# Eight small bias loads issued from SyncE instead of GpSimd at the start of a perceiver block

## The chip, the cores and the metric

The kernel runs on one core of one Trainium2 chip. The metric is the device time of one execution in microseconds (us), as the median of several runs. Profiled executions are read through a trace in which PE is TensorE, PEld its weight loads, DVE VectorE, ACT ScalarE, POOL GpSimd and SP SyncE. A name that ends in q (SPq, POOLq) is an engine's own queue of instructions, from which DMAs are issued.

## What is computed

One layer in float32 over x of 16 x 64 x 256 and a context of 16 x 1601 x 256: cross-attention, self-attention with rotary positions, and a mixture of 8 experts with one expert for each token and a capacity of 128.

```python
x = x + xattn(layernorm(x), ctx, ctx, Wq, bq, Wk, bk, Wv, bv, Wo, bo)   # 16 heads of 16
x = x + attn(layernorm(x), Wqkv, bqkv, Wout, bout)                      # 16 heads, rotary
x = x + ffn(layernorm(x), wg, W, b)                                     # top 1 of 8 experts
```

The biases are not zero. The loads that the change moves bring four of them: `be`, the experts' bias (8 x 256), and parts of `brows`, which holds bv, bo, bqkv and bout one after the other.

## The kernel before

Each of the five engines runs a program of its own; they meet at semaphores alone. The cross-attention goes through 16 contexts, one after the other. For each, PE makes keys (eight units, `L790`, 6 matmuls each, 512 or 65 columns wide) and values (seven units, `L799`, up to 12 matmuls of 256 columns), as sums of three products of bf16 parts. A unit goes to one of four PSUM banks for the first context, of two after that, and a unit may start only when the one before it in its bank has been read out: for keys by ACT (`khigh`, L1191) and then DVE (`klow`, L1458). SP copies the key rows by DMA into `kstack` (L487, three loads for each of eight pairs of heads), PE multiplies them with the queries (`ps_front`, L822), DVE takes maxima (L1475); then come the scores (L850), the exponentials (ACT, L1213), their low parts (POOL, L622) and the weighted values (L874).

The order on each engine is written out by hand as strings of letters (`PE_PROGRAM`, `ACT_PROGRAM`, `DVE_PROGRAM`, `POOL_PROGRAM`, and `FIRST_ORDER` for the units of the first context). Units 15 and 16 of the first context are the query tile 0 (its transposes L755, its product L765), unit 17 holds the transposes of query tile 1. PE runs 15, 16, then key units 0 to 5, unit 17, key unit 6, value units 8, 9, 10, and then the first two `ps_front` products.

What a query tile needs: DVE's moments (`query_moments` L1369, `query_variance` L1375 and L1377), then POOL's inverse root (L547) and normed rows `h0` (L551), then PE's transposes (L755). `mv0` and `h0` have one buffer each, so DVE's variance of the next tile waits for POOL's `h0` of this one (L1374), and POOL's next `h0` for PE's transposes. In the head, POOL does tile 0, the four quarters of the first context's low part (`clow`, L565), ten DMA issues (L572 to L580), and then tiles 1 and 2.

SP issues the loads of contexts and weights (L455 to L463), two loads of ones into rows 96 and 97 of `kstack` (L464, L465; each moves two rows of 25,632 bytes), then waits for the first query tile, writes it to DRAM (`q_blocks`, L471, two DMAs), waits until both have landed (`q_sent`, L478), and only then loads `qstack` (L480) and `kstack` (L487) in order.

The semaphore `ld_be` counts the eight small loads. It is waited for in `fold(0)` on POOL (L592; it runs after the first context's values, and the trace has it at 39.6 us), and by ACT in `rooms_empty` (L1227), after the sixteenth context. `ones_set` counts three fills by POOL, one of them that of `bias3` with zeros, into which six of the loads write.

Of the kernel before, what the change touches and what calls it, by code (L numbers as in the profile page):

```python
# [18 lines left out]
P = 128  # L19
D = 256  # L20
# [11 lines left out]
E = 8  # L32
# [178 lines left out]
def build(nc, x, ctxT, wqT, wkT, wvT, bqk, woT, wqkv, wout, brows, wg, weT, be, consts, ones2, out):  # L211
# [3 lines left out]
    with ctx:  # L215
        def sb(name, shape, dt=f32):
            return ctx.enter_context(nc.sbuf_tensor(name, shape, dt))

        def sem(name):
            return ctx.enter_context(nc.semaphore(name))  # L220
# [34 lines left out]
        bvcol = sb("bvcol", [P, 2, KT])  # L255
# [21 lines left out]
        bias3 = sb("bias3", [SEL, 3 * D])  # L277
# [75 lines left out]
        for rows, n in ((stats, 6), (mv, 2), (ve, 1), (rs, 1)):  # L353
# [22 lines left out]
        ones_set, st0_rdy, mv0_rdy, var0_rdy, rs0_rdy, bq4_rdy = (  # L376
            sem(n) for n in ("ones_set", "st0_rdy", "mv0_rdy", "var0_rdy", "rs0_rdy", "bq4_rdy"))
# [30 lines left out]
        ld_be, picked_rdy, pick_rdy, bias_rdy, wrot_rdy, we_rdy, vbd_set = (  # L408
            sem("t_" + n) for n in ("ld_be", "picked", "pick", "bias", "wrot", "we", "vbd"))
# [43 lines left out]
        def _(sp):  # L453
# [9 lines left out]
            sp.dma_start(cbuf[1][:, :, :], ctxT[1].rearrange("(k p) n -> p k n", p=P)).then_inc(c_loaded[1], 16)  # L463
            sp.dma_start(kstack[0][96:98, :, :].rearrange("p a n -> p (a n)").bitcast(f32), ones2).then_inc(ld_ones, 16)  # L464
            sp.dma_start(kstack[1][96:98, :, :].rearrange("p a n -> p (a n)").bitcast(f32), ones2).then_inc(ld_ones2, 16)  # L465

            def send_queries(t):

                wait_free(sp, [query_unit(t, NREAL + 1)])
                for n in range(2):  # L470
                    sp.dma_start(q_dram[n, 2 * t:2 * t + 2].rearrange("b p n -> p b n"),  # L471
                                 qbd[n][:, :, :].rearrange("p (b o) c -> p b (o c)", o=KT)).then_inc(q_sent, 16)
# [64 lines left out]
        def _(pool):  # L537
# [30 lines left out]
            for quarter in range(4):  # L568
                low_context(0, quarter)

            for r in range(3):
                pool.dma_start(bias3[32 * r:32 * r + E, 2 * D:3 * D], be).then_inc(ld_be, 16)  # L572
                pool.dma_start(bias3[32 * r:32 * r + 1, 0:2 * D],
                               brows[2 * D:4 * D].rearrange("(p n) -> p n", p=1)).then_inc(ld_be, 16)
            pool.dma_start(bvcol[:, 0, :], brows[0:D].rearrange("(k p) -> p k", p=P),
                           allow_slow_non_contiguous=True).then_inc(ld_be, 16)
            pool.dma_start(bvcol[:, 1, :], brows[4 * D:5 * D].rearrange("(k p) -> p k", p=P),
                           allow_slow_non_contiguous=True).then_inc(ld_be, 16)
            pool.dma_start(wqkv_sb[:, :, :], wqkv.rearrange("(k p) n -> p k n", p=P)).then_inc(ld_t, 16)
            pool.dma_start(wg_sb[:, :, :], wg.rearrange("(k p) n -> p k n", p=P)).then_inc(ld_t, 16)  # L580

# [34 lines left out]
            def low_prob(b, k):  # L616
                _, n = keys_of(k)
                i = NCH * b + k
                slot = i % NPAR
                pool.wait_ge(exp_done, 2 * (i + 1))  # L620
                wait(pool, pv_done, i - NPAR + 1)
                nc.gpsimd.tensor_tensor(plow[slot][0:n, :], prob[slot][0:n, :], p_high(slot, 0, HP * P)[0:n],  # L622
                                        ALU.subtract).then_inc(plow_gps, 1)
# [523 lines left out]
        def _(act):  # L1147
# [55 lines left out]
            def exponentials(b, h):  # L1203
                k, e = divmod(h, 2)
                _, nn = keys_of(k)
                i = NCH * b + k
                slot = i % NPAR
                act.wait_ge(score_done, 2 * NCH * b + h + 1)
                if h == 0 and b == 0:
                    act.wait_ge(v0_low, VUNITS)  # L1210
                if e == 0:
                    wait(act, pv_done, i - NPAR + 1)
                nc.scalar.activation(prob[slot][0:nn, e * 512:e * 512 + 512], ps_score[0:nn, h % NSB, :], ACT.Exp)\  # L1213
                    .then_inc(exp_done, 1)
# [143 lines left out]
        def _(dve):  # L1358
# [80 lines left out]
            def low_prob(b, k):  # L1439
                _, nn = keys_of(k)  # L1440
                i = NCH * b + k
                slot = i % NPAR
                dve.wait_ge(exp_done, 2 * (i + 1))
                wait(dve, pv_done, i - NPAR + 1)
                nc.vector.tensor_tensor(plow[slot][0:nn, :], prob[slot][0:nn, :], p_high(slot, 0, HP * P)[0:nn],
                                        ALU.subtract).then_inc(plow_dve, 1)
# [22 lines left out]
            def maximum(b, m):  # L1469
                dve.wait_ge(m_done, MUNITS * b + m + 1)  # L1470
                ps = ps_front[:, front_pos(m) % 2, :]
                unit = max_unit(m)
                _, hp, n = unit[0]
                _, nn = piece(n)
                nc.vector.reduce_max(maxes[:, hp:hp + len(unit), n],  # L1475
                                     ps[:, 0:len(unit) * nn].rearrange("p (h k) -> p h k", k=nn), AX.X).then_inc(m_free, 1)
                if m % (MUNITS // 2) == MUNITS // 2 - 1:
                    shift(b, m // (MUNITS // 2))
# [339 lines left out]
```

## Time and profile before

| | us |
|---|---|
| median of 3 runs | 725.64 |
| lowest, highest | 723.0, 725.91 |
| the profiled execution, its own time | 724.36 |
| its span, first to last instruction | 722.2 |
| mean granted TensorE clock | 0.991 |

Times in rows count from the span's start. In a timeline, a row is the start, the duration, the engine, the line and the operation; what stands in brackets is how long the engine sat idle before it and which work ended that. In the chain of work that ended last, a row is a start, a duration and what ran; it is followed back from the last instruction to the first. PEclk is the granted TensorE clock as a share of 2.4 GHz.

### The profile page before, as it was taken

The numbers are of one execution on the slowest core, as the hardware profiler recorded it, in microseconds if no ns is written. First come the engines' busy times: TensorE is split into PE (matmuls) and PEld (weight loads), VectorE is DVE, ScalarE is ACT, GpSimd is POOL, SyncE is SP. The second block draws the span as 40 slices with busy tenths as digits, with TensorE's granted clock in tenths as the row PEclk, the third lists the DMA queues.
The fourth block names the chain that finished last, engine by engine and source line by source line (L and its number), as shares of the span: only waits on it lengthen the run. The fifth ranks groups of instructions, "written<-read, shape, count | busy, mean of one in ns | idle before, by whom it ended". The sixth has DMA issues, their size and how long they took to land.

```text
span 722.2 us, 21443 instructions
## 1 busy us (share of the span) xinstructions
PE 679.1 (94%) x8591; PEld 514.8 (71%) x8647; DVE 540.3 (75%) x1110; ACT 449.9 (62%) x881; POOL 557.2 (77%) x378
## 2 busy tenths in 40 slices
PE   4889999999999999999999999999999998898796
PEld 2547776868776878687868786878686886676573
DVE  5598778868877887788768776877686978777636
ACT  2436765766666667666766666666666786666430
POOL 7986997999698969896989698869885789622313
PEclk9999999999999999999999999999999999999889
DMA  9486054444754354445444445454444330000124
GB/s 312 126 228 187 21 131 144 113 134 94 221 135 147 90 155 108 146 95 157 107 146 100 147 104 153 100 150 105 148 96 108 87 119 2 1 1 9 52 74 131
DMA packets 45658, 84.57 MB, mean 117 GB/s; under 512 B 8525, under 2 KB 28405, under 8 KB 45557
## 3 DMA queue, kind: packets, MB, share of 16 engines
q1 hardware_dynamic: 43848, 80.26, 40.7%
q0 software_dynamic: 1008, 2.40, 1.1%
q8 instruction: 69, 1.13, 0.7%
q10 hardware_dynamic: 704, 0.55, 0.3%
q14 instruction: 29, 0.23, 0.1%
HBM read 37.02 MB, written 6.82 MB: 61 GB/s over the span
## 4 chain that ended last, share of the span: by engine, by line
PE 79%; POOL 6%; issue 5%; DVE 5%; ACT 2%; DMA 2%; SPq 0%; POOLq 0%; DVEq 0%; ACTq 0%
PE ps_kv L799 17%; PE ps_kv L790 16%; PE ps_out L874 11%; PE ps_score L850 11%; PE ps_front L822 11%; POOL plow L622 3%; POOL clow L565 1%; PE ps_score L898 1%; PE ps_out L890 1%; PE ps_kv L898 1%; DVE klow L1458 1%; DVE maxes L1475 1%; PE ps_front L831 1%; PE ps_front L898 1%; DMA kstack<-khigh 1%
## 5 line engine op out<-in xcount | busy, mean ns | idle before, releaser
L622 POOL TENSOR_TENSOR plow<-prob 128x1024 bf16<-128x1024 f32 (+1 forms) x200 | 376.2, 1901 | 63.2 <-ACT prob L1213 60.7
L1475 DVE TENSOR_REDUCE maxes<-ps_front 128x1 f32<-128x512 f32 (+1 forms) x416 | 268.3, 665 | 70.7 <-PE ps_front L822 68.8
L1213 ACT ACTIVATE prob<-ps_score 128x512 f32<-128x512 f32 (+1 forms) x416 | 231.7, 595 | 48.1 <-PE ps_out L874 29.9
L850 PE MATMUL ps_score<-qstack,kstack 98*128 98x128 bf16 (+1 forms) x1664 | 140.1, 219 | 0.9 <-ACT prob L1213 0.7
L874 PE MATMUL ps_out<-vstack,prob 128*128 128x65 bf16 (+1 forms) x1664 | 137.9, 194 | 1.0 <-POOL plow L622 0.6
L850 PEld LDWEIGHTS ps_score<-qstack,kstack 98*128 98x128 bf16 (+1 forms) x1664 | 111.1, 98 | 38.6 <-ACT prob L1213 1.6
L874 PE MATMUL ps_out<-vstack,plow 128*128 128x65 bf16 (+1 forms) x1664 | 137.0, 192 | 0.0
L822 PE MATMUL ps_front<-kstack,qstack 96*128 96x512 bf16 (+1 forms) x512 | 135.7, 333 | 1.0 <-DMA kstack<-khigh 0.6
L874 PEld LDWEIGHTS ps_out<-vstack,prob 128*128 128x128 bf16 (+1 forms) x1664 | 118.5, 97 | 2.8 <-POOL plow L622 1.5
L874 PEld LDWEIGHTS ps_out<-vstack,plow 128*128 128x128 bf16 (+1 forms) x1664 | 112.7, 98 | 3.5
L1191 ACT ACTIVATE khigh<-ps_kv,bcol 128x512 bf16<-128x512 f32 (+1 forms) x123 | 72.9, 594 | 63.1 <-PE ps_kv L790 62.1
L565 POOL TENSOR_TENSOR clow<-cbuf 128x801 bf16<-128x801 f32 (+1 forms) x64 | 96.9, 1532 | 17.6 <-DMA cbuf<-in_ctxT 8.0
L799 PE MATMUL ps_kv<-w_hi,cbuf 128*128 128x256 bf16 (+1 forms) x402 | 109.6, 273 | 0.3 <-DVE vstack L1465 0.3
L799 PE MATMUL ps_kv<-w_hi,clow 128*128 128x256 bf16 (+1 forms) x402 | 109.5, 272 | 0.0
L799 PE MATMUL ps_kv<-w_lo,cbuf 128*128 128x256 bf16 (+1 forms) x402 | 109.4, 272 | 0.0
L1458 DVE SCALAR_TENSOR_TENSOR klow<-ps_kv,bcol,khigh 128x512 bf16<-128x512 f32 (+1 forms) x123 | 76.1, 629 | 40.1 <-ACT khigh L1191 39.9
L1199 ACT CAST vstack<-ps_kv 128x512 bf16<-128x512 f32 (+1 forms) x105 | 58.3, 556 | 71.6 <-PE ps_kv L799 71.1
L790 PE MATMUL ps_kv<-clow,w_hi 128*128 128x512 bf16 (+1 forms) x245 | 78.2, 332 | 4.6 <-DVE klow L1458 2.0
L790 PE MATMUL ps_kv<-cbuf,w_lo 128*128 128x512 bf16 (+1 forms) x246 | 80.6, 340 | 0.2 <-issue 0.2
L1465 DVE TENSOR_TENSOR vstack<-ps_kv,vstack 128x512 bf16<-128x512 f32 (+1 forms) x105 | 67.4, 643 | 0.2
L790 PE MATMUL ps_kv<-cbuf,w_hi 128*128 128x512 bf16 (+1 forms) x201 | 63.4, 331 | 2.8 <-DVE klow L1458 2.8
L822 PEld LDWEIGHTS ps_front<-kstack,qstack 96*128 96x128 bf16 x512 | 44.5, 97 | 17.0 <-DVE maxes L1475 2.8
(277 smaller groups left out, 844.6 us busy)
## 6 DMA issues: line engine op xcount, KB each, us to landing
kstack<-khigh SPq DMA_DIRECT2D x256, 100.1 KB, 2.2
cbuf<-in_ctxT SPq DMA_DIRECT2D x15, 1601.0 KB, 7.7
kstack<-klow SPq DMA_DIRECT2D x128, 100.1 KB, 2.2
qstack<-q_blocks SPq DMA_DIRECT2D x48, 64.0 KB, 2.7
q_blocks<-qbd SPq DMA_DIRECT2D x16, 128.0 KB, 2.0
cbuf<-in_weT SPq DMA_DIRECT2D x2, 1024.0 KB, 7.2
slot_x<-att_all SPq DMA_DIRECT2D x1, 1024.0 KB, 10.5
vstack<-slot_x SPq DMA_DIRECT2D x4, 256.0 KB, 3.5
```

What stands on the lines that cost most here:

```text
L565: nc.gpsimd.tensor_tensor(clow[par][:, k, a:a + n], cbuf[par][:, k, a:a + n], c_high(par, k, a, n), ALU.subtract).then_inc(clow_done, 1)
L622: nc.gpsimd.tensor_tensor(plow[slot][0:n, :], prob[slot][0:n, :], p_high(slot, 0, HP * P)[0:n], ALU.subtract).then_inc(plow_gps, 1)
L790: mm = nc.tensor.matmul(ps[:, 0:nn], w[0][:, k, t * P:(t + 1) * P], rhs, start=(j == 0), stop=(j == len(terms) - 1))
L799: mm = nc.tensor.matmul(ps[0:nn, a * D:(a + 1) * D], lhs, w[1][:, k, :], start=(j == 0), stop=(j == len(terms) - 1))
L822: mm = nc.tensor.matmul(ps[:, at:at + nn], qstack[par][0:96, q_at(hp), :], kstack[par][0:96, hp, n0:n0 + nn], start=True, stop=True)
L850: mm = nc.tensor.matmul(ps_score[0:nn, h % NSB, j * P:(j + 1) * P], kstack[par][0:98, hp, n0:n0 + nn], qstack[par][0:98, q_at(hp), :], sta ...
L874: mm = nc.tensor.matmul(o, lhs, vstack[par][0:nn, k, hp, 0:OW], start=(k == 0 and part == 0 and hp % 4 == 0), stop=(k == NCH - 1 and part ...
L1191: nc.scalar.activation(khigh[:, t, n0:n0 + nn], kv_bank(b, u)[:, 0:nn], ACT.Identity, bias=bcol[:, 1, t:t + 1]).then_inc(high_done, 1)
L1213: nc.scalar.activation(prob[slot][0:nn, e * 512:e * 512 + 512], ps_score[0:nn, h % NSB, :], ACT.Exp)\
L1458: nc.vector.scalar_tensor_tensor(klow[:, t, n0:n0 + nn], kv_bank(b, u)[:, 0:nn], bcol[:, 1, t:t + 1], khigh[:, t, n0:n0 + nn], ALU.add, AL ...
L1465: nc.vector.tensor_tensor(v[:, :, :, 32:64], kv_bank(b, u)[0:rows, 0:nch * D].rearrange("p (c h d) -> p c h d", c=nch, h=HP), v[:, :, :, 0 ...
L1475: nc.vector.reduce_max(maxes[:, hp:hp + len(unit), n], ps[:, 0:len(unit) * nn].rearrange("p (h k) -> p h k", k=nn), AX.X).then_inc(m_free, 1)
```

## The change

POOL no longer issues the six loads into `bias3` and the two into `bvcol`; SP issues them, after the loads of ones and before it waits for the first query tile. SP gets a wait for `ones_set`, so that `bias3` has been filled before. Semaphores, bytes and consumers stay as they were. The loads of `wqkv_sb` and `wg_sb` remain on POOL. Lines after 465 have numbers 9 higher in the kernel after, and those after 578 one higher.

```diff
@@ SP @@
             sp.dma_start(kstack[1][96:98, :, :].rearrange("p a n -> p (a n)").bitcast(f32), ones2).then_inc(ld_ones2, 16)
+            sp.wait_ge(ones_set, 3)
+            for r in range(3):
+                sp.dma_start(bias3[32 * r:32 * r + E, 2 * D:3 * D], be).then_inc(ld_be, 16)
+                sp.dma_start(bias3[32 * r:32 * r + 1, 0:2 * D],
+                             brows[2 * D:4 * D].rearrange("(p n) -> p n", p=1)).then_inc(ld_be, 16)
+            sp.dma_start(bvcol[:, 0, :], brows[0:D].rearrange("(k p) -> p k", p=P),
+                         allow_slow_non_contiguous=True).then_inc(ld_be, 16)
+            sp.dma_start(bvcol[:, 1, :], brows[4 * D:5 * D].rearrange("(k p) -> p k", p=P),
+                         allow_slow_non_contiguous=True).then_inc(ld_be, 16)
@@ GpSimd, after low_context(0, quarter) @@
-            for r in range(3):
-                pool.dma_start(bias3[32 * r:32 * r + E, 2 * D:3 * D], be).then_inc(ld_be, 16)
...
-            pool.dma_start(bvcol[:, 1, :], brows[4 * D:5 * D].rearrange("(k p) -> p k", p=P),
-                           allow_slow_non_contiguous=True).then_inc(ld_be, 16)
             pool.dma_start(wqkv_sb[:, :, :], wqkv.rearrange("(k p) n -> p k n", p=P)).then_inc(ld_t, 16)
```

On POOL before, from the first context's low part (`clow`) to the normed rows (`h`) of query tile 1, the instructions in their order are:

```order
L565 TENSOR_TENSOR clow<-cbuf 128x800 x2
L572 DMA bias<-in_be 8x256
L573 DMA bias<-in_brows 1x16x32
L572 DMA bias<-in_be 8x256
L573 DMA bias<-in_brows 1x16x32
L572 DMA bias<-in_be 8x256
L573 DMA bias<-in_brows 1x16x32
L575 DMA bvcol<-in_brows 128x2x1
L577 DMA bvcol<-in_brows 128x2x1
L579 DMA wqkv_sb<-in_wqkv 128x2x768
L580 DMA wg_sb<-in_wg 128x2x8
L547 TENSOR_TENSOR rs<-ve,half_neg 128x1
```

and on POOL now, at the same place:

```order
L574 TENSOR_TENSOR clow<-cbuf 128x800 x2
L580 DMA wqkv_sb<-in_wqkv 128x2x768
L581 DMA wg_sb<-in_wg 128x2x8
L556 TENSOR_TENSOR rs<-ve,half_neg 128x1
L560 TENSOR_SCALAR h<-x_all,mv,rs 128x256
```

Eight issues have left POOL, and the load of `wqkv_sb` comes right behind the low part. On SP now, between the loads of ones and the write of the first query tile (before, the first row was followed at once by the last two):

```order
L465 DMA kstack<-in_ones 2x6408
L468 DMA bias<-in_be 8x256
L469 DMA bias<-in_brows 1x512
L468 DMA bias<-in_be 8x256
L469 DMA bias<-in_brows 1x512
L468 DMA bias<-in_be 8x256
L469 DMA bias<-in_brows 1x512
L471 DMA bvcol<-in_brows 128x2x1
L473 DMA bvcol<-in_brows 128x2x1
L480 DMA q_blocks<-qbd 128x2x256 x2
L489 DMA qstack<-q_blocks 32x4x256 x3
```

The eight issues now stand in SP's queue ahead of `q_blocks`.

## Rows read from the trace of the kernel before

**Rows 1.** The page: busy us of the engines; the chain's shares by engine.
```profile
PE 679.1 (94%) x8591; PEld 514.8 (71%) x8647; DVE 540.3 (75%) x1110; ACT 449.9 (62%) x881; POOL 557.2 (77%) x378
...
PE 79%; POOL 6%; issue 5%; DVE 5%; ACT 2%; DMA 2%; SPq 0%; POOLq 0%; DVEq 0%; ACTq 0%
```
**Rows 2.** The chain that ended last, 0 to 60 us: start, duration, what.
```profile
13.77 0.74 POOL bias L572
...
28.63 1.31 PE ps_kv L799 x12
...
47.66 1.34 PE ps_kv L790 x6
```
**Rows 3.** Timeline of POOL, 0 to 25 us: start, duration, line, operation.
```profile
13.71 0.79 POOL L572 DMA_DIRECT2D bias<-in_be  x1
...
18.79 0.74 POOL L579 DMA_DIRECT2D wqkv_sb<-in_wqkv  x1
...
20.22 0.62 POOL L547 TENSOR_TENSOR rs<-ve,half_neg 128x1 f32<-128x1 f32 x1
20.95 1.22 POOL L551 TENSOR_SCALAR h<-x_all,mv,rs 128x256 f32<-128x256 f32 x1
```
**Rows 4.** Timeline of DVE, 17 to 23 us.
```profile
17.18 0.15 DVE L1377 TENSOR_SCALAR ve<-mv 128x1 f32<-128x1 f32 x1
...
22.27 0.18 DVE L1375 BATCH_NORM_AGGREGATE mv<-st 128x2 f32<-128x6 f32 x1 [3.29 <-POOL h L551]
...
22.56 0.28 DVE L1458 SCALAR_TENSOR_TENSOR klow<-ps_kv,bcol,khigh 128x65 bf16<-128x65 f32 x1
```
**Rows 5.** Timeline of PE, 19 to 30 us.
```profile
19.57 0.39 PE L790 MATMUL ps_out<-cbuf,w_lo 128*128 128x512 bf16 x1
22.22 0.44 PE L755 MATMUL ps_kv<-cst,h 128*128 128x128 f32 x2 [2.26 <-POOL h L551]
...
29.78 0.60 PE L822 MATMUL ps_front<-kstack,qstack 96*128 96x512 bf16 x2
```
**Rows 6.** Timeline of SP's queue, 0 to 26 us: its DMA issues.
```profile
3.66 3.03 SPq L463 DMA_DIRECT2D cbuf<-in_ctxT  x1
...
7.15 0.24 SPq L465 DMA_DIRECT2D kstack<-in_ones  x1
14.90 0.91 SPq L471 DMA_DIRECT2D q_blocks<-qbd  x2
21.95 1.28 SPq L480 DMA_DIRECT2D qstack<-q_blocks  x3
...
24.55 1.23 SPq L487 DMA_DIRECT2D kstack<-khigh  x2
```
**Rows 7.** SP's waits, 14 to 24 us: for what, total, times, longest.
```profile
SPq L480 <- DMA q_blocks<-qbd: 6.1, 1, 6.1
```
**Rows 8.** The page's DMA issues: count, KB each, us from issue to landing.
```profile
kstack<-khigh SPq DMA_DIRECT2D x256, 100.1 KB, 2.2
```
**Rows 9.** DMA answer of 0 to 40 us: the load of wqkv_sb.
```profile
wqkv_sb<-in_wqkv POOLq DMA_DIRECT2D x1, 768.0 KB, 4.7
```
**Rows 10.** DMA answer of 14 to 16 us: packets, what all queues moved.
```profile
DMA packets 130, 0.83 MB, mean 416 GB/s; under 512 B 0, under 2 KB 0, under 8 KB 130
```
**Rows 11.** DMA answer of 17.5 to 19.8 us: packets, MB, share of 16 engines.
```profile
q1 hardware_dynamic: 4, 0.05, 12.4%
```
**Rows 12.** The same view, POOL's queue, 16.2 to 17.6 us.
```profile
q0 software_dynamic: 128, 0.02, 8.4%
```
**Rows 13.** The same view, POOL's queue, 18.8 to 19.8 us.
```profile
q0 software_dynamic: 35, 0.00, 22.9%
```
**Rows 14.** By stretch: busy of PE, PEld, DVE, ACT, POOL; PEclk, DMA, GB/s.
```profile
22.80:26.20 3.40, 2.99 (x9) 1.36 (x11) 2.02 (x6) 0.73 (x2) 3.30 (x4) 0.50 0.64 160
26.20:29.80 3.60, 3.60 (x35) 3.23 (x34) 1.08 (x2) 2.38 (x5) 3.60 (x3) 1.00 0.63 148
```
**Rows 15.** Engines by stretch, the same columns, 36.0 to 45.7 us.
```profile
36.00:45.70 9.70, 7.52 (x46) 3.72 (x46) 9.56 (x24) 4.12 (x9) 7.46 (x9) 1.00 0.74 164
```

More of the change, by code:

```diff
@@ L569, in _ @@
                 low_context(0, quarter)
-            for r in range(3):
-                pool.dma_start(bias3[32 * r:32 * r + E, 2 * D:3 * D], be).then_inc(ld_be, 16)
-                pool.dma_start(bias3[32 * r:32 * r + 1, 0:2 * D],
-                               brows[2 * D:4 * D].rearrange("(p n) -> p n", p=1)).then_inc(ld_be, 16)
-            pool.dma_start(bvcol[:, 0, :], brows[0:D].rearrange("(k p) -> p k", p=P),
-                           allow_slow_non_contiguous=True).then_inc(ld_be, 16)
-            pool.dma_start(bvcol[:, 1, :], brows[4 * D:5 * D].rearrange("(k p) -> p k", p=P),
-                           allow_slow_non_contiguous=True).then_inc(ld_be, 16)
             pool.dma_start(wqkv_sb[:, :, :], wqkv.rearrange("(k p) n -> p k n", p=P)).then_inc(ld_t, 16)
```

## The prediction

> **What bounds the kernel now.** I read the page first. PE is busy for 679.1 us, and the chain of work that ended last is PE in 79% of the span and POOL in 6% [rows 1]. So time is won or lost where PE waits, and it has to be a wait in the head, since the change touches nothing else. Next, the chain in order of time. Behind POOL's four `clow` pieces it runs through POOL's DMA issues [rows 2], and these end only when POOL starts the inverse root for query tile 1 at 20.22 [rows 3]. DVE had the variance for it at 17.18 + 0.15 = 17.33 [rows 4]. Third, PE's timeline. Its key unit 5 ends at 19.57 + 0.39 = 19.96. Then it sits idle for 2.26 us until 22.22, until POOL's `h` (20.95 + 1.22 = 22.17) is there [rows 3, 5]. The small issues are the cause of that idle time.
>
> The next dependence on PE's path is the first `ps_front` product, at 29.78 [rows 5]. It wants `qstack` and the first head pair of `kstack`, which SP can ask for only when both writes of `q_blocks` have landed. SP issues these at 14.90, and waits 6.1 us for them, until 21.95 [rows 6, 7]. The third load of the first head pair starts its issue at 24.55 [rows 6] and lands some 2.2 us later [rows 8]: 26.75. Here the wait has 29.78 - 26.75 = 3.03 us of slack. That slack is what a faster POOL can use up; behind it stands a DMA queue.
>
> **What is removed.** Eight issues on POOL, from 13.71 to 18.79: 5.08 us [rows 3]. `wqkv_sb` and `wg_sb` follow in 20.22 - 18.79 = 1.43 us, so POOL is free for tile 1 at 13.71 + 1.43 = 15.14. It then waits for DVE, until 17.33. So of 5.08 us only 20.22 - 17.4 = 2.8 us move anything. The root and `h` take 22.17 - 20.22 = 1.95 us, and `h` is ready at 19.35, ahead of PE's 19.96. PE's idle 2.26 us goes entirely.
>
> **What PE does with it.** Unit 6 behind the transposes needs its bank, free after DVE's short `klow`, which stands in DVE's order behind a `mv` that waited 3.29 us for the old `h` [rows 4]. That `klow` ends at 22.84 before, 0.67 behind `h`; now at 19.35 + 0.67 = 20.02. The transposes take 0.44 [rows 5], so unit 6 starts at about 20.4. At full clock a key unit takes 1.34 and a value unit 1.31 [rows 2]: PE would reach the first `ps_front` at 20.4 + 1.34 + 3 x 1.31 = 25.7. That is 4.1 us earlier than 29.78; more than the 2.26 because units 6 and 8 ran at PEclk 0.50 from 22.8 to 26.2 in the trace [rows 14], behind the idle stretch that is gone. 4.1 us is the ceiling of the gain.
>
> **What holds it back.** If `q_blocks` landed as before, `kstack` would be there at 26.75 and the gain would be 3.0. But two things come ahead of it in the DMA engines.
>
> First, `wqkv_sb`: its issue moves from 18.79 to 13.71. Now its 768 KB [rows 9] run at 21 to 23.5 us, behind `q_blocks`; they will run from about 15 on, beside the second context and the two loads of ones. At the 416 GB/s of that stretch [rows 10] they are 786 / 416 = 1.9 us of every engine. In the stretch from 17.5 to 19.8 us SP's queue has two long packets (and two small ones), 12.4% of 16 engines, or 2 of 16 for 2.3 us [rows 11]: the loads of ones, on two engines alone, and `q_blocks` is complete only when these two engines have come to it. They have no gap in which to take 1.9 us more. I take the full 1.9; the bounds are 0 (another queue's packets slip in at no cost beside the slow long packets) and 1.9.
>
> Secondly, the small loads themselves, now ahead of `q_blocks` in SP's queue. The nearest rows are POOL's. With the six bias loads 128 packets took 8.4% of 1.4 us x 16, or 15 ns each [rows 12]; with the `bvcol` loads 35 packets took 22.9% of 1.0 x 16, or 105 ns each [rows 13]. The `bvcol` loads have 2 x 256 elements of 4 bytes, 32 for each engine. As packets of their own, they cost 32 x 15 ns = 0.5 us at the low end and 32 x 105 ns = 3.4 us at the high end. A packet of POOL's queue may hold many elements, so an element should cost far less than 105 ns, and those 15 ns are a mean over packets of up to 1 KB. I take 0.2 us, and keep 0 to 3.4 for the range.
>
> The Trainium skill, "DMA: Bandwidth & Descriptors", section "Rules for kernel authors", says that a strided last dimension is lowered to one descriptor per element, and that spreading DMAs over issuing engines saves the sequencer's time alone. The trace agrees with the second (5.08 us of POOL's time, the same engines busy); no row here shows the first for SP's queue. By the first, the price would be between the two ends above.
>
> SP's own issue time is covered. Its slowest issue took 3.03 us while earlier loads were outstanding, and its last ends at 7.15 + 0.24 = 7.39; it is idle until 14.90 [rows 6]. Eight issues at POOL's own price are 5.08 us and end at 12.5; even with one more stall of 3.03 they end at 15.5, 0.6 us behind 14.90, and `q_blocks` would still queue behind the ones loads. The wait for `ones_set` is met by 2 us. Behind it stand only these loads and the query writes. The loads' consumers come at 39.6 us and near the end: no wait there.
>
> **The sum.** `q_blocks` has landed at 21.95 + 1.9 + 0.2 = 24.05, and the first head pair, 26.75 - 21.95 = 4.8 later, at 28.85. The first `ps_front` moves from 29.78 to 28.85: -0.9 us. But PE now idles from 25.7 to 28.85, 3.1 us, longer than the 2.26 us behind which the clock fell to 0.50 (1.2 GHz) for 3.4 us [rows 5, 14]. If it falls again, it falls where PE is the bound, and 3.4 us at half rate lose 1.7 us. Before, the same loss was in front of the wait; now it would be behind it. Bounds 0 to +1.7; I take +1.7. Sum: -0.9 + 1.7 = +0.8 us. From there all moves together: DVE is full from 36.0 to 45.7 (9.56 of 9.70 us) [rows 15], but its work starts with PE's `ps_front`, so it shifts and absorbs nothing. Profiled: 724.36 + 0.8 = 725.2; the profiled run is 1.3 below the median of 725.64, so the median becomes **726.4**.
>
> **Rivals.**
> *The clock stays up*, because 3 us of idle time do not always bring it down, or `q_blocks` is late by less and the idle time is short: then -0.9 at the full delay, -3.0 at none. 724.7 to 722.6. For it: long packets of ones use 25.6 KB / 2.3 us = 11 GB/s of an engine that reaches 26 (416 / 16), so others may slip by. Against it: the clock fell behind a shorter idle time.
> *Tiny packets are dear on SP's queue*: at 105 ns an element, `q_blocks` lands 1.9 + 3.4 = 5.3 late, `kstack` at 32.05, PE loses 2.3 plus 1.7 for the clock: +4.0, 729.6, slower. With the clock's 1.7 us it passes 0.5% (+3.6) from 3.0 us of delay beyond `wqkv_sb`, or 94 ns an element; with the clock up, gain turns into loss from 1.1 us, or 34 ns. For it: 4-byte writes took the dearest packets of the trace. Against it: those packets may be groups.
> *PE gains its whole 4.1 us*, because the product does not wait for `kstack` as I read it: 721.5. Against it: the code has the wait.
> *It does nothing*: the head is as before because other waits (banks, ACT) end last; 725.6.
>
> **Chances.** Forecast +0.8: 0.45. Clock stays or less delay: 0.33. Nothing: 0.10. Tiny packets: 0.08. All 4.1 us: 0.04. A measurement tells 0.5%, 3.6 us, from no change, and the first three lie within that. Faster by over 0.5% 0.05, within 0.5% 0.87, slower 0.08. The range reaches from 722.6 (the -3.0) to 728.6 (+3.0: an element's price up to 75 ns); outside it are the 4.1 us, and the last third of the dear elements, some 1 in 10 together, and as much again for the measurement.
>
> **What would show it.** In the trace of after: POOL's root for tile 1 at 17.4 and `h` by 19.4; no idle time of PE ahead of its second pair of transposes; PEclk 1.00 from 22.8 to 26.2; SP's first `qstack` issue at 24 and not at 21.95; PE idle ahead of the first `ps_front`, released by the `kstack` load, at 28.9; PEclk 0.50 for some 3 us behind it. The prediction is wrong if `qstack` is issued by 22 (then -3.0), or after 26 (then slower), or if the clock does not fall.

## The result and the profile after

The changed kernel takes 727.67 us (median of 22 runs, 725.64 to 729.54), beside 725.16 us for the kernel before in the same comparison (22 runs, 722.78 to 727.42). The ratio is 1.0038, with a 95% interval of 1.0029 to 1.0047: **2.75 us slower** (2.1 to 3.4); the two medians themselves are 2.51 us apart. That is less than the 0.5% named in the prediction, but the interval excludes no change. The profiled executions had spans of 722.2 us before and 723.5 us after.

The page of the kernel after, busy us of the engines and the chain's shares by engine, to be laid beside [rows 1]:

```profile
span 723.5 us, 21499 instructions
...
PE 683.7 (94%) x8647; PEld 514.5 (71%) x8647; DVE 540.5 (75%) x1110; ACT 450.2 (62%) x881; POOL 552.9 (76%) x370
...
PE 80%; POOL 4%; DMA 4%; issue 4%; DVE 4%; ACT 2%; SPq 1%; POOLq 0%; ACTq 0%; DVEq 0%
```

POOL has lost 8 instructions, 4.3 us of busy time and 2 points of the chain. DMA has gained 2 points. The chain says where. Here it is for the kernel after, from the write of the first query tile to the first head product (start, duration, what):

```profile
14.88 0.37 SPq L480
...
15.29 10.55 DMA q_blocks<-qbd
25.84 0.02 issue
25.86 0.34 SPq L489
...
28.46 2.20 DMA kstack<-khigh
30.66 0.14 issue
30.80 1.01 PE ps_front L823 x2
```

The chain before ran through POOL's issues here [rows 2]. Now it is one DMA of 10.55 us. The next three fences are timelines of the kernel after (start, duration, engine, line, operation, idle time before it and its releaser). POOL, where [rows 3] had the eight small issues and a root at 20.22:

```profile
13.68 0.98 POOL L580 DMA_DIRECT2D wqkv_sb<-in_wqkv  x1
...
17.40 0.57 POOL L556 TENSOR_TENSOR rs<-ve,half_neg 128x1 f32<-128x1 f32 x1 [1.96 <-DVE ve L1378]
18.08 1.22 POOL L560 TENSOR_SCALAR h<-x_all,mv,rs 128x256 f32<-128x256 f32 x1
```

SP's queue, beside [rows 6]:

```profile
7.47 0.27 SPq L468 DMA_DIRECT2D bias<-in_be  x1
...
9.74 0.47 SPq L473 DMA_DIRECT2D bvcol<-in_brows  x1
14.88 0.88 SPq L480 DMA_DIRECT2D q_blocks<-qbd  x2
25.86 1.28 SPq L489 DMA_DIRECT2D qstack<-q_blocks  x3
```

PE, beside [rows 5]:

```profile
19.78 0.38 PE L756 MATMUL ps_kv<-cst,h 128*128 128x128 f32 x2
...
25.27 0.27 PE L800 MATMUL ps_kv<-w_hi,clow 128*128 128x256 bf16 x1
30.80 1.01 PE L823 MATMUL ps_front<-kstack,qstack 96*128 96x512 bf16 x2 [5.26 <-DMA kstack<-khigh]
31.60 0.42 PE L800 MATMUL ps_kv<-w_hi,cbuf 128*128 128x256 bf16 x1
```

The transposes start at 19.78 with no idle time ahead. PE is through its units at 25.54 and then idle for 5.26 us. The product that started at 29.78 before now starts at 30.80. SP issues `qstack` at 25.86; before, it was 21.95 [rows 6]. The same engines by stretch (columns as in [rows 14]: busy of PE, PEld, DVE, ACT, POOL; granted clock, DMA share, GB/s):

```profile
21.00:25.80 4.80, 4.54 (x39) 3.62 (x37) 2.03 (x5) 3.07 (x6) 4.80 (x4) 1.00 0.14 38
25.80:30.80 5.00, 0.00 (x1) 0.03 (x1) 0.00 (x0) 0.85 (x2) 5.00 (x5) 1.00 0.48 121
30.80:34.20 3.40, 3.40 (x15) 2.12 (x16) 1.29 (x2) 0.00 (x0) 0.13 (x1) 0.51 0.67 156
```

The clock is whole (2.4 GHz) up to the idle time, and half (1.2 GHz) for 3.4 us behind it. The first row also shows that, for the 4.8 us before `q_blocks` has landed, the DMA engines are busy for 0.14, some 2 of 16.

SP's load of the third context waits for PE's progress and marks how much of the shift is left. Before, it was issued at 43.94 us, and a later context's load at 507.36. After:

```profile
46.69 0.49 SPq L502 DMA_DIRECT2D cbuf<-in_ctxT  x1
...
510.11 0.40 SPq L502 DMA_DIRECT2D cbuf<-in_ctxT  x1
```

Both stand 2.75 us later: 1.02 from the later product, 1.7 behind it. Nothing is absorbed in between. That the spans differ by only 1.3 us comes from the end, where PE falls to half clock in stretches that differ from execution to execution. The stretch from 665 to 705 us, before and then after:

```profile
665.00:705.00 40.00, 33.59 (x300) 25.03 (x303) 19.10 (x64) 17.19 (x45) 10.82 (x14) 0.87 0.19 66
```

```profile
665.00:705.00 40.00, 33.18 (x309) 24.89 (x307) 20.92 (x74) 19.24 (x51) 10.97 (x14) 0.91 0.18 60
```

So below, each kernel is read by three things and, where they leave something out, by that later context's load: the issue of `qstack` (Q, the moment `q_blocks` has landed), the start of the first `ps_front` (PF), and the issue of the third context's load (C). Before: Q 21.95, PF 29.78, C 43.94. After: 25.86, 30.80, 46.69. From PF to C it is 14.16 us before and 15.89 after. C does not hold every wait of the first contexts: in two kernels below (e8 and e9) it comes too early for the whole of a wait at 39 to 41 us to show in it.

### The profile page after: what moved, and what is told of

Its sections match the earlier page's. It is cut to its first block, busy times and chain, and to the rows that moved or that the text cites. A ratio compares the mean times of both kernels' runs of the same rounds, so it can differ in the third digit from the quotient of the medians.

```text
span 723.5 us, 21499 instructions
## 1 busy us (share of the span) xinstructions
PE 683.7 (94%) x8647; PEld 514.5 (71%) x8647; DVE 540.5 (75%) x1110; ACT 450.2 (62%) x881; POOL 552.9 (76%) x370
## 3 DMA queue, kind: packets, MB, share of 16 engines
q1 hardware_dynamic: 44446, 80.29, 40.5%
## 4 chain that ended last, share of the span: by engine, by line
PE 80%; POOL 4%; DMA 4%; issue 4%; DVE 4%; ACT 2%; SPq 1%; POOLq 0%; ACTq 0%; DVEq 0%
PE ps_kv L800 17%; PE ps_kv L791 16%; PE ps_out L875 12%; PE ps_score L851 11%; PE ps_front L823 11%; POOL plow L623 3%; DMA q_blocks<-qbd 1%; PE ps_score L899 1%; PE ps_kv L899 1%; PE ps_out L891 1%; DMA kstack<-khigh 1%; PE ps_front L832 1%; DMA att_all<-in_wkT 1%; PE ps_front L899 1%; ACT kstack L1247 1%
## 5 line engine op out<-in xcount | busy, mean ns | idle before, releaser
L791 PE MATMUL ps_kv<-cbuf,w_hi 128*128 128x512 bf16 (+1 forms) x246 | 80.4, 340 | 3.2 <-DVE klow L1459 2.5
```

The source lines that it names most:

```text
L791: mm = nc.tensor.matmul(ps[:, 0:nn], w[0][:, k, t * P:(t + 1) * P], rhs, start=(j == 0), stop=(j == len(terms) - 1))
```

## The experiments

Q is 3.91 us late where the prediction had 2.1. Two **suspects** were new ahead of `q_blocks`: the load of `wqkv_sb`, and the eight small loads on SP. A third thing was there before too: the two loads of ones, whose long packets lie on two engines alone [rows 11]. In the first reading each suspect costs its bytes or its packets, and the two add up to 3.9. In the other (called W2 in the expectations) the two engines with the ones packets carry the whole delay, and what comes ahead of `q_blocks` is dear only there. A second question is what the half clock costs.

**Small loads ahead, `wqkv_sb` not** (`e1_w_late`). POOL issues the two weight loads behind query tile 2.

```diff
-            pool.dma_start(wqkv_sb[:, :, :], wqkv.rearrange("(k p) n -> p k n", p=P)).then_inc(ld_t, 16)
-            pool.dma_start(wg_sb[:, :, :], wg.rearrange("(k p) n -> p k n", p=P)).then_inc(ld_t, 16)
...
-            for letter in program(POOL_PROGRAM):
+            for at, letter in enumerate(program(POOL_PROGRAM)):
+                if at == 2:
+                    pool.dma_start(wqkv_sb[:, :, :], wqkv.rearrange("(k p) n -> p k n", p=P)).then_inc(ld_t, 16)
+                    pool.dma_start(wg_sb[:, :, :], wg.rearrange("(k p) n -> p k n", p=P)).then_inc(ld_t, 16)
```

> The kernel after, but GpSimd issues the loads of wqkv_sb and wg_sb behind the normed rows of query tile 2 (at about 21.8 us, not 13.7). The eight small loads stay on SyncE ahead of q_blocks. Theory W (the early wqkv_sb load on the same 16 engines is what delays q_blocks): of the 3.9 us by which the first qstack issue is late, at least 3 go, it stands at 22 to 23 us, the first ps_front at 26.8 to 27.8, and the kernel is 2.0 to 3.0 us faster than before. Theory S (the small loads ahead in SyncE's queue are the cause): the qstack issue stays at 24.5 us or later, the first ps_front at 29.4 or later, and the time is 0 to 2.5 us above before.

Measured 1.0042 (1.0025 to 1.0058). Q is 22.66: the small loads' price is small. But the product starts later than in any other kernel:

```profile
31.77 1.01 PE L824 MATMUL ps_front<-kstack,qstack 96*128 96x512 bf16 x2 [5.39 <-DMA kstack<-khigh]
```

In its chain the `kstack` load, 2.20 us in the kernel after, takes

```profile
26.42 5.22 DMA kstack<-khigh
```

`wqkv_sb`, issued at 22.47, now runs beside the `kstack` loads. The wait has only moved. C is 48.27, 4.3 us later than before, and the later context's load 4.6 later (512.00), where the timed runs are 1.8 to 4.2 us slower.

**`wqkv_sb` ahead, small loads not** (`e2_smalls_behind`). The eight loads stand behind the first query write on SP.

```diff
-            sp.wait_ge(ones_set, 3)
-            for r in range(3):
-                sp.dma_start(bias3[32 * r:32 * r + E, 2 * D:3 * D], be).then_inc(ld_be, 16)
...
             send_queries(0)
+            sp.wait_ge(ones_set, 3)
+            for r in range(3):
+                sp.dma_start(bias3[32 * r:32 * r + E, 2 * D:3 * D], be).then_inc(ld_be, 16)
...
             for b in BATCHES:
```

> The kernel after, but SyncE issues the eight small loads behind the two writes of q_blocks, not ahead of them. The early load of wqkv_sb stays. Theory W: the qstack issue stays late, at 24.8 us or later, and the time is 1.5 to 2.7 us above before. Theory S: the qstack issue goes back to 22 to 23 us, the first ps_front to 26.8 to 27.8, and the kernel is 2.0 to 3.0 us faster than before. If the two need each other (each small load takes its turn with a packet of wqkv_sb), both this and the kernel with the late wqkv_sb recover more than half of the 3.9 us.

Measured 1.0036 (1.0017 to 1.0056). Its SP queue and its PE:

```profile
24.77 1.30 SPq L479 DMA_DIRECT2D qstack<-q_blocks  x3
```

```profile
29.72 1.01 PE L822 MATMUL ps_front<-kstack,qstack 96*128 96x512 bf16 x2 [3.51 <-DMA kstack<-khigh]
```

The product starts where it did before (29.78), yet C is 46.88. Its stretches from 30 us, to be compared with 0.94 in the kernel after from 34 to 36:

```profile
30.00:32.00 2.00, 2.00 (x9) 1.18 (x8) 1.29 (x2) 0.00 (x0) 1.54 (x2) 0.50 0.69 162
...
34.00:36.00 2.00, 2.00 (x11) 1.41 (x10) 1.04 (x2) 0.40 (x1) 1.13 (x1) 0.51 0.29 69
```

The half clock held until 36 us here, 6.3 us from the product's start against 3.4 in the kernel after. From PF to C it is 17.16 us, 3.0 more than before. The stretch behind an idle time is not of one length.

**Neither ahead** (`e3_both_behind`): both edits together.

```diff
             send_queries(0)
+            sp.wait_ge(ones_set, 3)
+            for r in range(3):
...
+                if at == 2:
+                    pool.dma_start(wqkv_sb[:, :, :], wqkv.rearrange("(k p) n -> p k n", p=P)).then_inc(ld_t, 16)
...
```

> The kernel after with both moves: the small loads behind q_blocks on SyncE, and wqkv_sb and wg_sb behind query tile 2 on GpSimd. By W and by S alike nothing new stands ahead of q_blocks: qstack issue at 21.5 to 22.0 us, first ps_front at 26.4 to 26.9 us instead of 29.78, TensorE idle for some 1 us ahead of it and its clock up; 2.8 to 3.3 us faster than before. If the time does not fall by at least 2 us, the head is not what sets the time, and both theories are wrong.

Measured 1.0061 (1.0033 to 1.0088): the expectation is missed by far. Q is right, PE is not:

```profile
21.40 1.30 SPq L479 DMA_DIRECT2D qstack<-q_blocks  x3
```

```profile
29.88 0.59 PE L823 MATMUL ps_front<-kstack,qstack 96*128 96x512 bf16 x2 [4.45 <-DMA kstack<-khigh]
```

Chain and stretch of this kernel show what took the gain:

```profile
24.46 5.28 DMA kstack<-khigh
```

```profile
24.00:28.00 4.00, 1.43 (x14) 1.03 (x11) 0.00 (x0) 2.15 (x4) 4.00 (x4) 1.00 0.99 291
```

All 16 engines are full (0.99) with 768 KB that PE does not need yet, while `kstack` takes 5.28 us. With e1 this says: between `q_blocks` and `kstack` there was one free slot, and the kernel before had `wqkv_sb` in it. The time is less well explained than the wait. C is 45.70, 1.8 us later than before, and the later context's load 2.4 later (509.74), where the six timed runs are 2.4 to 6.4 us slower.

The runs so far also answer half of the first question: Q is 21.40 with nothing ahead, 22.66 with the small loads (+1.26), 24.77 with `wqkv_sb` (+3.37), 25.86 with both (+4.46). The prices nearly add up, but 3.37 us is more than 768 KB take at the 416 GB/s of [rows 10] (1.9).

**The loads of ones away** (`e4_ones_late`). All else as after.

```diff
-            sp.dma_start(kstack[0][96:98, :, :].rearrange("p a n -> p (a n)").bitcast(f32), ones2).then_inc(ld_ones, 16)
-            sp.dma_start(kstack[1][96:98, :, :].rearrange("p a n -> p (a n)").bitcast(f32), ones2).then_inc(ld_ones2, 16)
...
                 keys(b)
+                if b == 0:
+                    sp.dma_start(kstack[0][96:98, :, :].rearrange("p a n -> p (a n)").bitcast(f32), ones2).then_inc(ld_ones, 16)
+                    sp.dma_start(kstack[1][96:98, :, :].rearrange("p a n -> p (a n)").bitcast(f32), ones2).then_inc(ld_ones2, 16)
```

> The kernel after, but the two loads of ones (25,632-byte rows, on two engines alone) are issued behind the first context's kstack loads instead of ahead of q_blocks. Both suspects stay: wqkv_sb early, small loads ahead of q_blocks. If the two engines with the long packets carry the whole delay (W2): the other 14 had their share done by about 20.8 us, so qstack is issued at 20.5 to 21.5 us, the first ps_front at 25.5 to 26.3, and the kernel is 3.3 to 4.2 us faster than before. If all 16 engines are late because of the bytes of wqkv_sb (W1): qstack at 24 us or later and the time at or above before.

Measured 0.9959 (0.9946 to 0.9971), 3.0 us faster than before. Its SP queue, its PE, and its engines up to Q:

```profile
20.19 1.28 SPq L487 DMA_DIRECT2D qstack<-q_blocks  x3
```

```profile
26.28 0.59 PE L824 MATMUL ps_front<-kstack,qstack 96*128 96x512 bf16 x2 [0.61 <-DMA kstack<-khigh]
```

```profile
15.30:20.20 4.90, 4.90 (x30) 2.31 (x28) 4.44 (x13) 2.27 (x4) 3.00 (x4) 1.00 0.88 309
```

Both suspects are still ahead of `q_blocks`, and Q falls by 5.67 us. The engines are now busy for 0.88 up to the landing, where the kernel after ended with 4.8 us at 0.14. So W2 holds: the two engines with the ones packets carry the delay. C is 40.45, 3.5 us earlier than before.

**The same on the kernel before** (`e6_before_ones`), to see whether the ones loads were what bound it: the same edit on the kernel before.

```diff
                 keys(b)
+                if b == 0:
+                    sp.dma_start(kstack[0][96:98, :, :].rearrange("p a n -> p (a n)").bitcast(f32), ones2).then_inc(ld_ones, 16)
...
```

> The kernel before with the loads of ones behind the first context's kstack loads. GpSimd still issues the eight small loads. If in the kernel before the first ps_front waits for TensorE's own work (idle 2.26 us for query tile 1, then half clock) and not for kstack, nothing is gained: within 0.7 us of before, though qstack is issued 2 us or more earlier. If q_blocks already ended last in before, the time falls by 1.5 us or more.

Measured 1.0007 (0.9992 to 1.0022): nothing. Q is 17.95, four microseconds earlier, and PF 29.85, because PE still waits for POOL:

```profile
22.18 0.44 PE L756 MATMUL ps_kv<-cst,h 128*128 128x128 f32 x2 [2.26 <-POOL h L552]
```

Neither removing POOL's issues (the change) nor removing the ones packets (this) helps alone; together they bring 3.0 us.

**`wqkv_sb` where nothing runs** (`e7_w_gap`): as e3, but the weight loads stand among the first values.

```diff
+                if at == 10:
+                    pool.dma_start(wqkv_sb[:, :, :], wqkv.rearrange("(k p) n -> p k n", p=P)).then_inc(ld_t, 16)
...
```

> Small loads on SyncE behind q_blocks, wqkv_sb and wg_sb issued by GpSimd among the first values, at 31 to 34 us, where the queues are empty. In the kernel with both moves the wqkv_sb load met the kstack loads. If wqkv_sb costs wherever it meets q_blocks or the first kstack loads, and nothing elsewhere: qstack issue at 21.4 us, kstack lands at 26.2, first ps_front at 26.3 us, clock up, 3.0 to 3.8 us faster than before. If something else holds kstack back, the first ps_front stays at 29 us or later and the time at or above before.

Measured 0.9979 (0.9966 to 0.9992), or 1.5 us faster than before. Q is 21.31.

```profile
26.97 0.59 PE L823 MATMUL ps_front<-kstack,qstack 96*128 96x512 bf16 x2 [1.46 <-DMA kstack<-khigh]
```

The wait is 1.46 us, the clock stays whole, and C is 41.28 (-2.7). That confirms what e3's loss was; the gain in time fell short of the 3.0 to 3.8 us expected, while the trace came near to it. The next run asks whether the loads of ones cost what is left of the wait.

**The same with the ones loads away too** (`e8_w_gap_ones`): e7 and e4 together.

```diff
+                if at == 10:
+                    pool.dma_start(wqkv_sb[:, :, :], wqkv.rearrange("(k p) n -> p k n", p=P)).then_inc(ld_t, 16)
...
+                if b == 0:
+                    sp.dma_start(kstack[0][96:98, :, :].rearrange("p a n -> p (a n)").bitcast(f32), ones2).then_inc(ld_ones, 16)
...
```

> As the kernel with wqkv_sb in the empty stretch, and the loads of ones behind the first context's kstack loads. Nothing is left ahead of q_blocks but the second context: qstack at 18 to 20 us, kstack bound by DVE's short klow or by SyncE's issues, first ps_front at 25.5 us with no idle time of TensorE ahead of it: the whole 4.1 us of the prediction's ceiling, 3.8 to 4.5 us faster than before. If the ceiling is mis-read, it stops at 3 us, as with the ones late alone.

Measured 0.9993 (0.9976 to 1.0009). Q is 18.67, and PE now has no wait at all:

```profile
25.29 0.60 PE L824 MATMUL ps_front<-kstack,qstack 96*128 96x512 bf16 x2
...
39.22 0.41 PE L792 MATMUL ps_kv<-cbuf,w_hi 128*128 128x512 bf16 x1 [2.66 <-DVE klow L1460]
```

The product starts 4.5 us earlier than before, so the ceiling of 4.1 us is reached, and what the ones loads cost in e7 is gone. But part of the gain is given back at 39 us: that wait was 1.31 us in the kernel after, and the clock falls to 0.64 in the mean from 40 to 44 us behind it. C, at 39.46, is still 4.5 us earlier than before; the later context's load, at 505.40, is only 2.0 earlier, and the time 0.5 us (1.7 faster to 0.7 slower). DVE's rows show what ended later:

```profile
34.84 1.75 DVE L1430 CAST tri_bf<-cst 128x128 bf16<-128x128 f32 x1
```

The cast takes 0.38 us in e4, 1.37 us less, and the wait is 1.35 us longer than in the kernel after. POOL's two issues in the middle of its copies (31.88 to 33.6) push these copies (`vstack`) to 36.5, beside DVE's cast. That the copies are the reason is read from the rows; no run moved the cast or the copies alone.

**POOL issues the small loads, but late** (`e9_pool_behind`): ones away, `wqkv_sb` early as in e4, the eight loads back on POOL behind query tile 2. This asks whether SP as the issuer matters, or only their place.

```diff
-                sp.dma_start(bias3[32 * r:32 * r + E, 2 * D:3 * D], be).then_inc(ld_be, 16)
...
+                if at == 2:
+                    for r in range(3):
+                        pool.dma_start(bias3[32 * r:32 * r + E, 2 * D:3 * D], be).then_inc(ld_be, 16)
...
```

> The ones loads behind the first context's kstack loads, as before in the fast kernel, but the eight small loads are back on GpSimd, behind query tile 2 and not ahead of tile 1. wqkv_sb is issued early, as in the kernel after. If all that counts is that nothing small stands ahead of GpSimd's tile 1 and nothing long ahead of q_blocks' last packets: qstack issue at 18.5 to 20.5 us, first ps_front at 25.3 to 26.3 us, 2.5 to 4 us faster than before, the same as with the small loads on SyncE. If it takes SyncE (5 us of issues on GpSimd delay the second context's low part until TensorE waits for it): less than 1.5 us faster, with TensorE idle for clow.

Measured 1.0025 (1.0009 to 1.0041). Q is 19.75 and PF 26.62, nearly e4's. DVE and PE later:

```profile
36.16 1.70 DVE L1429 CAST tri_bf<-cst 128x128 bf16<-128x128 f32 x1
37.78 1.10 DVE L1430 TENSOR_TENSOR mask<-cst 128x4 f32<-128x4 f32 x1
...
39.53 1.07 DVE L1437 CAST pick<-picked 72x1024 bf16<-72x1024 f32 x1
```

```profile
41.41 0.39 PE L791 MATMUL ps_kv<-cbuf,w_hi 128*128 128x512 bf16 x1 [3.54 <-DVE klow L1459]
```

The eight issues keep POOL from 21.68 to 26.38 and its copies run until 39.4, where e4's ended at 36.1. There the casts took 0.38 and 0.69, and the mask between them 0.59:

```profile
35.82 0.38 DVE L1430 CAST tri_bf<-cst 128x128 bf16<-128x128 f32 x1
...
37.35 0.69 DVE L1438 CAST pick<-picked 72x1024 bf16<-72x1024 f32 x1
```

Together the three are 2.2 us longer here, and so is the wait (3.54 us against 1.30 in e4). The expectation had named a wait for `clow`; this one is for `klow`. PE's clock did not fall behind it (the stretch from 40 to 44 us; the one from 38 to 40, without work for PE, has 1.00 too):

```profile
40.00:44.00 4.00, 2.53 (x18) 1.15 (x18) 3.93 (x10) 0.90 (x2) 3.76 (x5) 1.00 0.83 226
```

The later context's load is at 506.49, 0.9 us earlier than before, and yet the timed runs are 0.7 to 3.0 us slower than before. That difference stays open. Between e9 and e12 (below), which has the eight loads on SP behind the first query write, lie 0.62% of time and 3.1 us at the later context's load. So the change's own idea, SP in place of POOL, is worth something once the queue is clear, at least against this place on POOL; another place on POOL was not tried. The two were timed on different chips, each beside the kernel before.

**The clock's price** (`e5_warm`, and `e10_warm24` with 24): dummy products keep PE busy ahead of the wait. They are work added, and write a bank that the real product overwrites.

```diff
+                if b == 0 and m == 0:
+                    for _ in range(20):
+                        nc.tensor.matmul(ps, w_hi[0][:, 0, 0:P], c_high(0, 0, 0, 512), start=True, stop=True)
                 if m == 0:
                     pe.wait_ge(q_loaded, 48 * (b + 1))
```

> The kernel after, and TensorE does 20 matmuls more (512 columns each, w_hi on the first context, into the ps_front bank that the first product then overwrites) ahead of its wait for the first kstack load: at 0.22 us each they fill 4.4 of the 5.3 us in which it sat idle. Nothing waits for them. If 1.7 us of the slowdown are the halved clock behind that idle time, the clock stays at 2.4 GHz (PEclk 1.00 from 31 to 35 us), the first ps_front stays at 30.8 us, and the kernel is 1.5 to 1.9 us faster than after, 0.8 to 1.3 us above before. If the halved clock costs nothing (DVE or kstack end last there), the time is that of after, 2.7 us above before.

Measured 1.0032 (1.0018 to 1.0046). Its PE:

```profile
25.40 4.69 PE L819 MATMUL ps_front<-cbuf,w_hi 128*128 128x512 bf16 x20
30.75 0.59 PE L826 MATMUL ps_front<-kstack,qstack 96*128 96x512 bf16 x2 [0.66 <-DMA kstack<-khigh]
```

The same start as after (30.80), but 0.59 us in place of 1.01, and C at 44.90: from PF to C 14.15 us, as before, and 1.7 less than after. In time only 0.4 us of it is seen, with an interval of about 1.2 either way, so the 1.5 to 1.9 us expected are missed. More runs follow, with 24 products and beside them the kernel after (`e11_after_again`, no edit).

```diff
-                    for _ in range(20):
+                    for _ in range(24):
```

> As the kernel with 20 more matmuls ahead of TensorE's wait, but 24, which fill the whole 5.3 us. The trace of the first put the later context loads 1.8 us ahead of those of after, but its timed runs only 0.4 us (by 1.2 either way). If 1.7 us are the halved clock: faster than the kernel after timed beside it by 1.2 to 2.2 us, and the second context load issued at 44.7 to 45.2 us. If the halved clock costs nothing in the end: within 0.5 us of it.

> The kernel after, timed on the same chip beside the one with 24 more matmuls: 2.2 to 3.3 us above before. Its profile shows how the end of the kernel varies between executions: if the span's difference to the first profile of after (723.5 us) comes from the stretches of 1.2 GHz behind 670 us, the time up to 510 us agrees within 0.5 us and only the end differs.

Measured 1.0019 (1.0004 to 1.0033) and 1.0046 (1.0030 to 1.0062), 0.27% apart, or 2.0 us; with these intervals about 1.5 us either way (the medians are 1.5 us apart). The kernel after had Q 25.82, PF 30.77 and C 46.91 again, 16.14 us from PF to C. With the 24 products, which last beyond the landing of `kstack`, PF was 31.48 and C 45.65, 14.17 us. In the traces the price of the half clock is 1.7 to 2.0 us; the timed runs agree with that in direction and bound its size only loosely.

**The best of the parts** (`e12_best`): ones away, small loads on SP behind the first query write, `wqkv_sb` early.

```diff
-            sp.dma_start(kstack[0][96:98, :, :].rearrange("p a n -> p (a n)").bitcast(f32), ones2).then_inc(ld_ones, 16)
...
             send_queries(0)
+            sp.wait_ge(ones_set, 3)
+            for r in range(3):
...
                 keys(b)
+                if b == 0:
+                    sp.dma_start(kstack[0][96:98, :, :].rearrange("p a n -> p (a n)").bitcast(f32), ones2).then_inc(ld_ones, 16)
...
```

> The ones loads behind the first context's kstack loads, the eight small loads on SyncE behind the writes of q_blocks, wqkv_sb early on GpSimd as in the kernel after. Against the kernel with the ones late alone it takes the small loads out of q_blocks' way (they were worth 1.3 us of delay in the kernels with the ones ahead), and it keeps GpSimd free of issues behind query tile 1. Theory: qstack issue at 19 to 19.7 us, first ps_front at 25.4 to 25.9 us (TensorE's own limit), DVE's tri_bf cast at 0.4 us and not 1.7; 3.0 to 4.2 us faster than before. If the small loads cost nothing once the ones are gone: the same as with the ones late alone, 3.0 us.

Measured 0.9963 (0.9948 to 0.9978), 2.7 us faster than before. Q is 19.75. Its PE:

```profile
25.82 0.59 PE L823 MATMUL ps_front<-kstack,qstack 96*128 96x512 bf16 x2 [0.32 <-DMA kstack<-khigh]
```

C is 39.97, 4.0 us earlier than before, and e4's was 3.5 earlier; their times can't be told apart. Both beat both kernels. Why 1.3 us of the trace's gain is missing in the time stays open; the half-clock stretches at the end, which differ from execution to execution, are one candidate.

## Why the prediction was nearly right, and the step that failed

**Right, POOL and PE.** Root at 17.4 (forecast 17.4), `h` at 19.30 (19.35), no idle time ahead of the transposes, full clock up to the wait, PE there at 25.54 (25.7). That e8 starts the product at 25.29 shows the ceiling of 4.1 us to have been real.

**Right, the wait that follows.** PF is released by `kstack`, which lands 4.80 us behind Q (25.86 to 30.66), as forecast. PE's idle time is 5.26 us (3.1), the clock falls, for 3.4 us, and costs 1.7; the traces of e5, e10 and e11 confirm the term, the timed runs only loosely. The shift of 2.75 us passes unabsorbed to 510 us.

**Wrong, a term's size: what stands ahead of `q_blocks`.** The sum had 2.1 us in front of Q against the trace's 3.9, and with it -0.9 for PF where +1.0 was measured. That is all of the miss: +1.0 + 1.7 = 2.7 against -0.9 + 1.7 = 0.8. The step that failed is that `wqkv_sb` costs its bytes at the rate of all engines, 1.9 us, *and that this was called the upper bound*. It measured 3.37 (e3 to e2), or 3.2 with the small loads there too (e1 to after, 22.66 to 25.86). With the small loads that makes 4.46 us from e3 to after; the kernel before itself was 0.55 us behind e3 (21.95 against 21.40), which leaves the 3.91. The prediction had seen that the two engines with the ones packets end last, and then priced the load on them by a mean over 16. By e4, e8 and e12 the price depends on the ones packets:

| ahead of `q_blocks` | Q with ones | Q without ones |
|---|---|---|
| nothing (e3; e8) | 21.40 | 18.67 |
| `wqkv_sb` (e2; e12) | 24.77 | 19.75 |
| `wqkv_sb` and small loads (after; e4) | 25.86 | 20.19 |

Without ones `wqkv_sb` costs 1.1 us and the small loads 0.4; with them 3.4 and 1.1. The trace of the kernel after shows two parts of the 3.4. These are its queues from 21.7 to 24.0 us, where the engines are nearly idle but for two (packets, MB, share of 16 engines, as in [rows 11]; q0 is POOL's queue, q1 is SP's):

```profile
q0 software_dynamic: 22, 0.09, 10.6%
q1 hardware_dynamic: 77, 0.03, 4.7%
```

POOL's queue has only `wqkv_sb` and the 8 KB of `wg_sb` left here. It takes 10.6% of 2.3 us x 16, or 1.95 us on each of two engines, behind the long packets of ones and beside SP's, among which are those of `q_blocks`. So the bytes do cost some 1.9 us, but on the engines that end last and after the long packets. The second part is in the long packets themselves: two of them took 2.3 us each before [rows 11], and in the kernel after, in the view of 18.0 to 18.5 us, 73.2% of 0.5 us x 16, or 2.9 us each. What makes up the rest of the 3.4 us, and in which order the packets of the two queues take turns on an engine, stays open.

That those two loads use two engines is the trace's reading (12.4% of 16 in [rows 11], 0.14 after). The Trainium skill, "DMA: Bandwidth & Descriptors", section "Why a DMA increments its semaphore by 16 and not by 1", says that a transfer is dealt to the largest number of engines, up to 16, that divides the slowest dimension of both its source and its destination, which for two rows is 2, and that for hardware queues such as SP's these are the lowest-numbered. The trace agrees on the number; which engines they are, no view here tells.

**The small loads.** Taken at 0.2 us with bounds 0 to 3.4, they measured 1.1 to 1.3 with the ones packets there. The bounds held; the value was too low, because the prediction let a packet hold many elements. On SP's queue it does not: that queue has 598 packets more on the page of the kernel after (44,446 against 43,848), of which the 2 x 256 elements of `bvcol` can be 512, while POOL's has 256 fewer (752 against 1,008). From 16 to 17 us, 510 packets under 512 bytes are seen. As an estimate, 1.1 to 1.3 us over 32 elements for each engine is at most 34 to 41 ns an element, between the prediction's 15 and 105. The *dear tiny packets* fell with that: 3.4 us would have put Q at 25.3 without `wqkv_sb` (e1 has 22.66). SP's issues took 0.25 to 0.47 us each and ended at 10.21, without a stall: covered, as forecast.

**The other rivals.** *The clock stays up* fell with the row at 0.51. *It does nothing* and *all 4.1 us* fell with Q and PF.

**Luck.** The time lay inside the range because the range reached up to +3.0 us, and that room had been kept for dear small packets. They used 0.9 us of it (1.1 against 0.2); the larger part of the excess, 1.5 us, was `wqkv_sb` beyond what had been called its upper bound. Q, at 25.86, stopped just short of the 26 us that the prediction had named as a sign of being wrong.

**Not seen at all.** That before held a good place for `wqkv_sb`, in the one free slot. The prediction counted what its earlier load costs `q_blocks`, and rightly had no gain from leaving the later slot. With the ones loads where they were, issuing it at 13.7 us (after, e2) and at 22 us (e1, e3) were both worse than the place before; only the one behind the first `kstack` loads (e7) was better.

## What to carry to other kernels

When an issue moves, list what it now overtakes in the DMA engines, and price it on the engine that ends last, not by bytes over the mean rate: a load of two long rows holds two engines while fourteen are idle. A load that nobody waits for soon still has one best place, which an unrelated edit can take away. Before removing a cause, look which resource becomes the next one: here the removal of POOL's issues and of the long packets did nothing or harm alone, and gave 3 us together.

## What the runs showed of the hardware

- The delay of one DMA behind long packets on two engines is not the sum of sizes: 768 KB of another queue cost `q_blocks` 3.4 us with them and 1.1 us without.
- A longer idle time of PE did not cost more. From the start of the product behind it, the half clock lasted 6.3 us behind 3.51 us of idle time (e2), 3.4 us behind 5.26 (after), and to 34.7 us, 3.9, behind 5.33 in the same kernel again (e11), where it had begun at 28 us, within the idle time. PF to C was longer by 3.0, 1.7 and 2.0 us, about half of each. Behind 2.66 us (e8) it fell; behind 3.54 us (e9) it did not, nor behind 0.3 to 1.5 us (e4, e7, e12).
- A DVE cast from fp32 to bf16 of 128x128 takes 0.38 us, or 1.70 to 1.75 beside POOL's `vstack` copies (e8, e9). The Trainium skill, "SBUF — State Buffer", section "Who interferes with whom", says that a DVE cast may use a port pair that GpSimd needs too, and that whichever issues first holds it for the whole instruction. The longer casts agree. But in e12 the cast starts at 35.36 while a smaller copy of POOL is recorded (35.01 to 35.66) and takes 0.38 all the same, and so it is in e4 (35.82, beside 35.47 to 36.12). So when the two collide is not settled by these runs.
